# A graph layer and a gated FFN on one core: scatters at 4.5 a group, the start reordered, and the graph biases added by GpSimd instead of by matmuls

## The reference

```
x1  = x + LN(x) @ W1.T + b1 + mean_over_edges(LN(x)[nbr]) @ W2.T + b2
out = x1 + shared_mlp(LN(x1)) + gated(top 2 of 4 expert MLPs of LN(x1))
```

## Time and profile before

| | us |
|---|---|
| median of 3 runs | 3266.72 (3265.14 to 3267.07) |
| the profiled execution, its own time | 3267.08 |
| its span | 3265.5 |
| PE busy in the span | 3104.3 (95%) |
| DVE busy | 2673.0 (82%) |
| ACT busy | 1944.1 (60%) |
| POOL busy | 1831.9 (56%) |

### The profile page before, as it was taken

How to read it: one execution, slowest core, us unless ns; L and a number is a source line. 1 busy time by engine, 2 the same in 40 slices (tenths; PEclk the granted TensorE clock), 3 DMA queues, 4 the chain that set the end, 5 groups by cost and what they waited for, 6 DMA issues and landing times.

```text
span 3265.5 us, 61478 instructions
## 1 busy us (share of the span) xinstructions
PE 3104.3 (95%) x20817; PEld 2846.7 (87%) x20817; DVE 2673.0 (82%) x7212; ACT 1944.1 (60%) x3507; POOL 1831.9 (56%) x1554
## 2 busy tenths in 40 slices
PE   6988889989949999999999999999999999999998
PEld 6988888889948888888888888888888888888987
DVE  7878878786438888888888888888888888888886
ACT  4655555555626656566665656666665656666565
POOL 1688888888445554555555555555555555555540
PEclk9998899999979999999999999999999999999999
DMA  8776666676643333333333333333333333333330
GB/s 247 205 186 180 178 195 180 177 198 179 180 126 89 97 93 89 98 84 99 85 100 92 91 97 84 97 83 101 90 94 98 85 98 84 99 87 97 93 82 26
DMA packets 201856, 387.38 MB, mean 119 GB/s; under 512 B 106703, under 2 KB 109853, under 8 KB 201538
## 3 DMA queue, kind: packets, MB, share of 16 engines
q1 hardware_dynamic: 133938, 226.03, 25.6%
q10 hardware_dynamic: 30800, 102.42, 9.8%
q0 software_dynamic: 36800, 54.95, 7.2%
HBM read 236.11 MB, written 161.00 MB: 122 GB/s over the span
## 4 chain that ended last, share of the span: by engine, by line
PE 70%; DVE 0%; ACT 0%; DMA 0%; POOL 0%; issue 0%; SPq 0%; POOLq 0%; DVEq 0%
PE acc L1129 25%; PE acc L1190 13%; PE acc L1099 12%; PE acc L1110 4%; PE acc L1112 4%; PE acc L1176 3%; PE acc L1153 3%; PE acc L1186 1%; PE acc L1145 1%; PE acc L1201 1%; PE acc L1139 1%; DMA tab<-tab_d 0%; POOL e_oh L178 0%; POOL rows L166 0%; ACT h2f L1234 0%
## 5 line engine op out<-in xcount | busy, mean ns | idle before, releaser
L166 POOL DMA_INDIRECT rows<-z_d,tab x500 | 568.1, 1136 | 645.2 <-DMA tab<-tab_d 486.0
L178 POOL TENSOR_SCALAR e_oh<-iota_sb,tab 128x250 fp32r<-128x250 f32 (+1 forms) x500 | 522.6, 1056 | 470.2 <-PE acc L1112 466.5
L1129 PE MATMUL acc<-x1T_hi,wl_hl 128*128 128x500 f32 x2400 | 665.4, 392 | 0.0
L387 POOL DMA_INDIRECT tab_d<-pair,idx x400 | 555.0, 1387 | 118.9 <-issue 104.7
L726 PE MATMUL acc<-w_hl,xT_hi 128*125 128x256 f32 x3200 | 586.6, 289 | 0.0
L1129 PEld LDWEIGHTS acc<-x1T_hi,wl_hl 128*128 128x128 f32 x2400 | 444.0, 188 | 84.0
L726 PEld LDWEIGHTS acc<-w_hl,xT_hi 128*125 128x125 f32 x3200 | 483.2, 195 | 0.0
L1190 PE MATMUL acc<-wl_hl,h_hi 128*125 128x256 f32 x2400 | 477.7, 281 | 0.0
L1391 DVE TENSOR_TENSOR h_lo<-h1f,h_hi 128x500 fp32r<-128x500 f32 x600 | 396.8, 674 | 49.1 <-ACT h_hi L1228 39.7
L1221 ACT ACTIVATE h1f<-acc,bl_sb 128x500 f32<-128x500 f32 x600 | 404.2, 674 | 14.4
L1190 PEld LDWEIGHTS acc<-wl_hl,h_hi 128*125 128x125 f32 x2400 | 390.6, 185 | 3.7
(11 more groups left out here) (145 smaller groups left out, 6400.8 us busy)
## 6 DMA issues: line engine op xcount, KB each, us to landing
xs<-in_x SPq DMA_DIRECT2D x100, 448.0 KB
z_d<-zs ACTq DMA_DIRECT2D x100, 448.0 KB
y_d<-ys ACTq DMA_DIRECT2D x100, 448.0 KB
y_sb<-y_d SPq DMA_DIRECT2D x100, 448.0 KB
x_sb<-in_x SPq DMA_DIRECT2D x100, 448.0 KB
out<-x_sb SPq DMA_DIRECT2D x100, 448.0 KB
codes_b<-code_d SPq DMA_DIRECT2D x25, 390.6 KB
rows<-z_d,tab POOLq DMA_INDIRECT x500
```

Of the source, the lines that this page charges most:

```text
L166: pool.indirect_dma_start(out=rows[g.h][:, q, :], out_offset=None, in_=z_d, in_offset=bass.IndirectOffsetOnAxis(ap=tab[g.h][:, q, 0:1], ax ...
L178: pool.tensor_scalar(e_oh[:, q, w], iota_sb[:, w], tab[g.h][:, q, 1:2].bitcast(F32), None, ALU.is_equal).then_inc(S["e_oh_ready"], 1)
L387: pool.indirect_dma_start(out=tab_d, out_offset=bass.IndirectOffsetOnAxis(ap=idx[:, n:n + 1], axis=0), in_=pair[:, 2 * n:2 * n + ROW], in_ ...
L1129: mm = pe.matmul(bank[L1_BANKS[t]][:, 0:GN], wl1_hl[:, w, f, t * P:(t + 1) * P], (x1T_hi, x1T_lo)[a][:, f, :], start=n == 0, stop=n == 5)
```

## The change

It has five parts.

1. In pass 1 the scatters go out at 4.5 a group (`9 // 2`) instead of 5, so they end in group 96 instead of 87. Three instead of two stand ahead of `rstd` in a group.
2. The four bias matmuls of each group in pass 1 are gone (400 in all), with their operands, the small DVE chain that made them and the DMA that moved one row of them across partitions.
3. Start of pass 1: DVE takes the statistics of the first two groups ahead of the edge arithmetic on the targets, PE transposes the edge arrays ahead of the first x group, the targets are loaded earlier, the fill of the table is spread over groups 0 to 4 between the loads of x, and the FFN's weights are loaded at groups 20 and 24.
4. `bias_rows` holds b1+b2 on 125 partitions. In pass 2 POOL adds it to the loaded rows of x, one instruction of 125x1024 a group (`x_and_bias`), at the end of its step, and DVE's `base_rows` waits for that (`xb_ready`) instead of for the loads.
5. In the second step of pass 2's lead-in (`i.c == -2`) the gather of group 2 stands behind the one-hots of group 1 and the first power, instead of ahead of them.

```
-                        for k in range(NFILL): ... fill DMAs ...   (all ahead of load_x(6))
-                        sp.wait_ge(s_bs, 7)
-                        sp.dma_start(bias_r[1:2].bitcast(F32), st_bl[:].bitcast(F32)).then_inc(s_row, 16)
...
+                            if 2 * g < NFILL:
+                                for k in (2 * g, 2 * g + 1):
+                                    sp.dma_start(fill_v[0][:, k * FILL:(k + 1) * FILL], fill[:])\
+                                      .then_inc(s_filled, 16)
...
-                                n = (g - G_SCAT) * PER_G
-                                for e in range(n, min(n + 2, EC)):
+                                n = min(EC, (g - G_SCAT) * 9 // 2)
+                                m = min(EC, (g + 1 - G_SCAT) * 9 // 2)
+                                for e in range(n, min(n + 3, m)):
                                     scatter(e)
                             if g % 2 == 0 and g + 4 < NG:
                                 rstd(g // 2 + 2)
                             if g >= G_SCAT:
-                                for e in range(n + 2, min(n + PER_G, EC)):
+                                for e in range(n + 3, m):
                                     scatter(e)
...
-                                if b == 2:
-                                    pe.matmul(o, two_ones[:], bias_r[:], start=True, stop=False)
...
-                        pe.wait_ge(s_bs, 8)
-                        pe.wait_ge(s_row, 16)
...
             def base_rows(dve, g):
-                wait_alone(dve, s_yl[g.h], g.half(2 * LOAD))
+                wait_alone(dve, S["xb_ready"], g.n(1, 1))
...
+            def x_and_bias(pool, g):
+                wait_alone(pool, s_yl[g.h], g.half(2 * LOAD))
+                pool.tensor_tensor(x_sb[g.h][:], x_sb[g.h][:],
+                                   bias_rows[:].unsqueeze(1).to_broadcast([SP_, NS, D]),
+                                   ALU.add).then_inc(S["xb_ready"], 1)
+
             def step_pool(pool, i):
-                if (i + 4).exists():
+                if (i + 4).exists() and i.c != -2:
                     gather(pool, i + 4)
                 if (i + 3).exists() and i.c > -3:
                     edges_onehots(pool, i + 3)
...
+                if i.c == -2:
+                    gather(pool, i + 4)
+                if (i + 3).exists():
+                    x_and_bias(pool, i + 3)
```

More of the change, by code:

```diff
@@ L59 @@
 NSC = 8
-PER_G = 5
 WINDOW = ((0, 2), (0, 2), (0, NS), (2, NS), (2, NS))
@@ L120, in build @@
                  "h1_relu_ready h1_hi_ready h1_lo_ready gate_bc_done l2_done h2_relu_ready "
-                 "h2_gated base_ready h2_hi_ready h2_lo_ready l3_done out_ready cleared").split()
+                 "h2_gated xb_ready base_ready h2_hi_ready h2_lo_ready l3_done out_ready cleared").split()
         S = {n: sem(n) for n in names}
@@ L353, in _ @@
                                 load_x(g + XB)
+                            if g == 0:
+                                sp.wait_ge(s_fillset, 3)
+                            if 2 * g < NFILL:
+                                for k in (2 * g, 2 * g + 1):
+                                    sp.dma_start(fill_v[0][:, k * FILL:(k + 1) * FILL], fill[:])\
+                                      .then_inc(s_filled, 16)
+                            if g == 20:
+                                sp.dma_start(st_wl1[:], wl1).then_inc(s_wl, 16)
+                                sp.dma_start(st_wl2[:], wl2).then_inc(s_wl, 16)
+                                sp.dma_start(st_wl3[:], wl3).then_inc(s_wl, 16)
+                            if g == 24:
+                                sp.dma_start(st_gw[:], gw).then_inc(s_wl, 16)
+                                sp.dma_start(st_b3[:], b3).then_inc(s_wl, 16)
+                                sp.dma_start(st_sel[:], selg).then_inc(s_wl, 16)
+                                sp.dma_start(iota_sb[:], iota).then_inc(s_cst, 16)
+                                sp.dma_start(bl1_sb[:], bl1).then_inc(s_cst, 16)
+                                sp.dma_start(bl2_sb[:], bl2).then_inc(s_cst, 16)
+                                sp.dma_start(gb_sb[:], gb.partition_broadcast(P)).then_inc(s_cst, 16)
+                                sp.dma_start(tie_sb[:], tie).then_inc(s_cst, 16)
                             if blocks < NCH // CB4 and CB4 * (blocks - 1) <= last_chunk(g) + 1:
@@ L727, in rows_of @@
                                                        w12_hl[:, w, f, wt],
-                                                       start=b == 4 and n == 0, stop=n == 5)
+                                                       start=n == 0, stop=n == 5)
                                         n += 1
@@ L746, in _ @@
                         pe.wait_ge(s_id, 16)
-                        transposes(0)
                         for a in range(4):
@@ L757, in _ @@
                             mm.then_inc(s_tr, 1)
+                        transposes(0)
                         pe.wait_ge(s_whi, 1)
                         pe.wait_ge(s_wlo, 1)
-                        pe.wait_ge(s_bs, 8)
-                        pe.wait_ge(s_row, 16)
                         pe.wait_ge(s_one, 1)
```

37 lines of the change are left out of this document (12 added, 25 removed).

## The result

| | us |
|---|---|
| kernel before, beside it | 3266.89 median (3265.14 to 3270.93, 4 runs) |
| kernel after | 3377.31 median (3376.44 to 3382.09, 4 runs) |
| ratio | 1.0339, 95% interval 1.0321 to 1.0357 |
| profiled execution after | 3382.09, its span 3380.5 |

The account below looks back on a forecast made before the run. POOL was taken to bound pass 1 and PE pass 2. The sum was 3267.1 - 64 (pass 1) - 6.5 (lead-in) + 175 (`x_and_bias`) = 3371 us, range 3215 to 3500, likeliest 3310 to 3480.

Parts of the forecast that it names:

- the likeliest case: Pass 2: PE stalls of 1.2 to 3 us a step, time 3310 to 3480; chance 0.57.
- What bounds each pass: Pass 1: POOL is saturated and ends last; pass 2: PE is busy all the time at full clock.
- Start, -14: Start of pass 1: first product at about 24.6 us, 13 us earlier, plus 1 us in groups 0 to 7.
- The bound: Start of pass 1: the fills compete with the loads of x, which could return 5 us of the gain.
- Last power at 820: End of POOL's pass 1 stream: 726 us from group 8's power, last power at 820 instead of 883.12; -63 with the start.
- The tail of pass 1, -1: Six groups behind the last power: missing bias matmuls shorten something if ACT keeps up, 0 to 4 us, taken as 1.
- Bias matmuls worth nothing: Pass 1: the 400 bias matmuls gain nothing for most of the pass, since POOL still ends last.
- Lead-in, -6.5: Lead-in of pass 2: first power moved ahead of group 2's gather, transposes at about 962 instead of 968.45.
- fits before DVE's need of it: Lead-in of pass 2: the next step's gather, one-hots and power, ending at 971, come before DVE needs them.
- `x_and_bias`, +175: Pass 2: POOL's 2.8 us addition holds DVE's two-SBUF-input instructions 2.26 us; PE stalls 1.80 us in 97 steps.
- the hidden addition: Rival, pass 2: DVE isn't held, or only briefly, and the step stays 22.9 us; 3197; chance 0.16.
- the costlier case: Rival, pass 2: addition over 4 us, or granted clock falls as PE idles (at 0.91, +213: 3584); chance 0.13.

Follow-up runs that it names:

- e5: Kernel before with its 400 bias matmuls left out, nothing else changed; 3262.41 us, ratio 0.9987.
- e6: Kernel before with scatters at 4.5 a group instead of 5, three ahead of the power; 3212.13 us, ratio 0.9834.
- e1 to e4: Changed kernel with POOL's pass 2 addition left out, replaced by a memset, halved, or moved: 3201.45, 3209.18, 3271.76, 3213.82 us.
- e8: Kernel before with the start part alone and the low bias row made on DVE without a DMA; 3260.70 us, ratio 0.9983.
- e10: Changed kernel with biases by matmul again and its ten table fills spread over seven groups' loads instead of five; 3197.78 us, ratio 0.9797.
- e1: Changed kernel without POOL's addition in pass 2, graph biases left out of the result; 3201.45 us, ratio 0.9797.
- e7: Changed kernel with biases by matmul in pass 1 again, low bias row made on DVE, no addition on POOL; 3195.45 us, ratio 0.9787.
- e4: Changed kernel with the same addition moved behind the gathers and DVE's second gating product, in steps with layers 1 to 3; 3213.82 us, ratio 0.9832.
- e2: Changed kernel with the addition replaced by a POOL memset of 2048 columns that reads no SBUF, biases left out; 3209.18 us, ratio 0.9821.

## Why the prediction was right

The forecast time is 6 us off the median (11 off the profiled execution, to which the sum was made), inside the likeliest case. By its own steps:

- **What bounds each pass**: right. e5 removes PE's work in pass 1 and gains 4 us; e6 shortens POOL's stream per group and gains 54.
- **Start, -14**: mis-sized, -7.25 at group 8, -9.1 to -9.9 in e1 to e4 and -5.7 in e8's time. The first product was forecast at 24.6 and came at 26.92, and the gain then shrank further. The bound (fills against loads, 5 of it given back) named a place. e10, which spread the fills, was 2.2 us ahead where they were thinned and lost it where they were put, so the bound is borne out in part; the rest of the shortfall has no cause shown.
- **Last power at 820**: it came at 828.61. The stream was forecast at 726 us and is 728.2 and, in e6, 726.3. Of the 8.6 us, 6.7 are the start's. With the start of e1 to e4 it came at 825.2 to 826.0.
- **The tail of pass 1, -1**: not settled. In this profile it is 30.4 us against 37.5, since a group less was left behind the last power. But the same pass 1 has 34 to 38 in e1 to e4, and up to 232 products left. Pass 1 in all was -61.6 here and -56.8 to -61.4 in e1 to e4, for a forecast of -64. Here that is an error of 6.7 us at the start which the short tail cancels by chance; in e1 it is a start of -9.9 and a tail of +0.4.
- **Bias matmuls worth nothing**: right for the pass (e5: 4 us in all; e7: no loss when they are put back).
- **Lead-in, -6.5**: first transposes at 900.00, 41.0 us behind the first gather instead of 47.8, so -6.8. But "fits before DVE's need of it" failed for the first step, once. DVE waits 1.84 us for that power, then an `x_and_bias` at 912.55 meets `x1n`, which takes 3.71 us instead of 1.38, and PE waits 3.93:

```profile
912.55 2.34 POOL L1468 TENSOR_TENSOR x_sb<-x_sb,bias_rows 125x1024 f32<-125x1024 f32 x1
912.60 3.71 DVE L1406 TENSOR_SCALAR x1n_sb<-x_sb,l_mv,l_rstd 125x256 f32<-125x256 f32 x4 [1.84 <-POOL l_rstd L1482]
...
916.94 1.20 PE L1083 MATMUL acc<-h_hi,wl_hl 128*128 128x500 f32 x2 [3.93 <-DVE h_lo L1375]
```

- **`x_and_bias`, +175**: the mechanism is right, shown from four sides (taken away, made to read nothing, halved, moved), and the steps behind the first cost 176.0. (That e1's 175.9 is the same number is partly chance: it holds the lead-in's 8.8 as well, less what pass 1 and the end happened to give.) The stall per step is the forecast 1.80 us to the hundredth, by four errors that cancel. The addition takes 2.39 us and not 2.8. DVE is held till 0.14 us before its end and not till 0.38, and meets it 0.11 us behind its start and not 0.16. The slack is 0.33 us and not 0.46. The estimate from the Trainium skill's page "GPSIMD Engine Reference" (section 3.1), 2.25 us, was nearer to 2.39 than my price from the one-hots. With my hold and slack it made 3318, since the other terms were off as well.
- **The rivals**: the hidden addition (3197) falls with the first profile; the clock stays at 1.00 in pass 2, so the costlier case falls too; pass 1 did speed up.

The parts, each alone on the kernel before, are -5.7 (start), -54.3 (scatters) and -9.9 (lead-in), together -69.9; all three at once, in e7, give -71.0. So 71 us of gain were lost, and 110 more, to one instruction of 2.39 us a step on an engine that was idle at the time.

## What to carry to other kernels

An idle engine is not a free one: before work goes to POOL's gaps, look at which DVE instructions with two SBUF inputs stand at that moment, how much slack the chain behind them has, and price hold less slack by the number of steps. If it must be there, put it where DVE's next results are needed late (e4), and look first whether the work it replaces was on the path at all (e5, e7). When one engine paces a pass, look also at how much is left to do behind its last instruction (e6), and take more than one profile of it: the same pass 1 ended 30.4 to 37.9 us behind its last power.

## What the runs showed of the hardware

- An addition on POOL with both inputs in SBUF took 1.28 us for 512 columns and 2.39 for 1024: 2.16 ns a column and 0.17 us besides. A `memset` on POOL took 1.80 us for 2048 columns, 0.88 ns each.
- DVE's addition of two SBUF tiles, begun 0.11 us behind POOL's, took 2.31 us. If it ran in its last 0.18 us, as long as it takes undisturbed, it overlapped the last 0.14 us of POOL's instruction.
- DVE's splits with one input in PSUM kept their 0.67 us beside the same addition on POOL (e4: at most 679 ns in 200 instructions), while the two with both inputs in SBUF took 2.51 us instead of 1.35.
- A `memset` on POOL left DVE's addition of two SBUF tiles at 0.18 us, and held a `tensor_scalar` on DVE (one SBUF tensor in, SBUF out): 1881 ns, median 408 (e2, once).
- With fills, loads and stores together on the DMA queues, ACT took 4.78 us to issue two stores of y at 42.63 us, 3.49 in e10 at 66.38, and 1.07 in e7 at 67.71.
- PE idling 23.4 of 500 us, in pieces of about half a us each step, left its granted clock at 1.00, its upper level, in all of that stretch. In pass 1 at 450 to 600 us, PE idled 8 to 26 us of 150 in the twelve profiles at a mean granted clock between 0.91 and 0.98, and e5, which idled most, had 0.91 as the kernel before had.
